# Query projection parts in every second slot of a turn, and row maxima stored ahead of the rotation

## The reference

```python
q = (x @ Wq).reshape(b, n, N_HEADS, HEAD_DIM)     # 32 heads of 16
k, v = jnp.split(ctx @ Wkv, 2, axis=-1)
...
q = apply_axial_rope(q, pos_map)
k = apply_axial_rope(k, ctx_pos_map)
logits = jnp.einsum('bqhd,bkhd->bhqk', q, k) * scale
w = jax.nn.softmax(logits, axis=-1)
attn = jnp.einsum('bhqk,bkhd->bqhd', w, v)
attn = attn.reshape(b, n, N_HEADS * HEAD_DIM)
return attn @ Wout + bout
```

## Time and profile before

| | us |
|---|---|
| median of 3 runs (1388.97 to 1389.15) | 1389.12 |
| the profiled execution's own time | 1388.06 |
| span of its profile | 1386.4 |
| attention: first scores at 721.84, last value products at | 1243.5 |
| one turn with c = 1 or 2 of batches 1 and 2 | 32.4 |
| TensorE busy, of the span | 1177.1 |
| VectorE busy | 856.9 |
| ScalarE busy | 653.6 |
| GpSimd busy | 414.5 |

### The profile page before, as it was taken

The page is one execution under the profiler, slowest core; times in us unless marked ns, Lnnn a source line. Parts: engine busy times, 40 slices in busy tenths (PEclk is TensorE's granted clock), DMA queues, the critical chain, the costliest instruction groups (busy, mean ns, idle before and its releaser), DMA issues.

```text
span 1386.4 us, 16598 instructions
## 1 busy us (share of the span) xinstructions
PE 1177.1 (85%) x5316; PEld 503.8 (36%) x5317; DVE 856.9 (62%) x1324; ACT 653.6 (47%) x1146; POOL 414.5 (30%) x479
## 2 busy tenths in 40 slices
PE   5875865999889999972459998999999999888898
PEld 3443432555444444431112222322332222234443
DVE  7899875314335555414697888777877777613543
ACT  2454452555312222232436675666666656663443
POOL 2575470011132222104333342233223223102332
PEclk8988888999989999995669999999999999999999
DMA  7223123434254444319633332222222225300011
GB/s 257 92 107 122 53 99 126 163 122 140 78 181 148 148 148 148 125 72 276 148 93 85 109 89 74 89 74 75 74 89 75 85 78 70 47 1 9 31 39 46
DMA packets 106357, 141.59 MB, mean 102 GB/s; under 512 B 20788, under 2 KB 75572, under 8 KB 106280
## 3 DMA queue, kind: packets, MB, share of 16 engines
q1 hardware_dynamic: 87432, 111.37, 24.6%
q0 software_dynamic: 18368, 28.85, 8.0%
q10 hardware_dynamic: 480, 0.39, 0.1%
HBM read 97.44 MB, written 46.27 MB: 104 GB/s over the span
## 4 chain that ended last, share of the span: by engine, by line
PE 30%; DVE 8%; issue 7%; ACT 6%; POOL 2%; DMA 2%; POOLq 0%; ACTq 0%; DVEq 0%
PE PS L2596 8%; PE PS L2566 6%; PE PS L2510 5%; PE PS L2534 5%; ACT a_E L2677 4%; PE PS L2583 4%; DVE a_top L2854 3%; POOL a_K L1908 1%; DMA a_attnT<-f_y,l_pos 1%; PE PS L2137 1%; DVE a_tab L1934 1%; DVE a_early L2756 1%; PE PS L2160 1%; PE PS L2506 0%; PE PS L2527 0%
## 5 line engine op out<-in xcount | busy, mean ns | idle before, releaser
L2854 DVE TENSOR_REDUCE a_top<-PS 128x2 f32<-128x1024 f32 x256 | 308.4, 1223 | 94.7 <-PE PS L2583 90.5
L2677 ACT ACTIVATE a_E<-PS 128x512 f32<-128x512 f32 x512 | 277.7, 596 | 148.2 <-PE PS L2566 147.9
L2566 PE MATMUL PS<-a_Q,a_K 99*128 99x512 bf16 (+1 forms) x512 | 168.0, 388 | 17.9 <-ACT a_E L2677 7.8
L1366 PE MATMUL PS<-f_W,f_GT 128*128 x312 | 141.6, 597 | 0.0
L2596 PE MATMUL PS<-a_E,a_V 128*32 128x512 f32 x1024 | 139.0, 615 | 0.0
L2583 PE MATMUL PS<-a_K,a_Q 64*128 64x512 bf16 x512 | 104.5, 405 | 39.4 <-DVE a_top L2854 25.8
L2566 PEld LDWEIGHTS PS<-a_Q,a_K 99*128 99x128 bf16 (+1 forms) x512 | 44.5, 98 | 154.6 <-ACT a_E L2677 102.3
L1770 POOL TENSOR_TENSOR a_qf<-a_qf,a_tab 128x512 f32<-128x512 f32 x15 | 19.0, 1268 | 268.9 <-DVE a_swapped L2778 268.9
L1422 DVE TENSOR_TENSOR f_H<-f_SG,PS 128x256 f32<-128x256 f32 x39 | 16.4, 421 | 125.0 <-ACT f_SG L1406 125.0
L1366 PEld LDWEIGHTS PS<-f_W,f_GT 128*128 128x128 f32 x312 | 56.9, 192 | 57.3 <-issue 57.3
L2510 PE MATMUL PS<-a_xT,a_early 128*128 128x512 f32 x128 | 75.6, 689 | 2.1 <-ACT a_xT L2647 0.8
(11 more groups left out here) (364 smaller groups left out, 2005.9 us busy)
## 6 DMA issues: line engine op xcount, KB each, us to landing
f0r_raw<-in_L_ffn_W_dram SPq DMA_DIRECT2D x24, 512.0 KB, 5.0
a_K<-k_parts SPq DMA_DIRECT2D x192, 64.0 KB, 2.3
a_Q<-a_q_parts SPq DMA_DIRECT2D x186, 64.0 KB, 2.5
f_y<-f_Y SPq DMA_DIRECT2D x39, 256.0 KB, 2.0
v_units<-V SPq DMA_DIRECT2D x16, 512.0 KB, 2.8
a_V<-v_units SPq DMA_DIRECT2D x16, 512.0 KB, 3.5
k_parts<-f_k_parts SPq DMA_DIRECT2D x16, 384.0 KB, 3.3
a_q_parts<-a_parts SPq DMA_DIRECT2D x16, 384.0 KB, 2.8
```

The lines of the kernel that those rows point to most:

```text
L1366: last = nc.tensor.matmul(PS[:, 2 + k % 2, 0:2 * I], GT[k][:, c, :], W13[:, bass.ds(e, 1), c, :].rearrange("p a n -> p (a n)"), start=(c = ...
L2566: nc.tensor.matmul(PS[:, 4 + h % 2, :], K6[k][0:rows_, o, head // 2, kt * P:(kt + 1) * P], Q6[k][0:rows_, o, head // 2, :], start=True, st ...
L2677: nc.scalar.activation(E[step % 2][:, h, :], PS[:, 4 + h % 2, :], ACT.Exp).then_inc(exp_done, 1)
L2854: nc.vector.tensor_reduce(top[:, h - h % 2:h - h % 2 + 2, t], PS[:, 2 * pair:2 * pair + 2, :], AX.X, ALU.max).then_inc(maxed, 1)
```

## The change

For the turns with c = 1 to 3, the parts of `q` move from the slots 0, 1, 2, 3 to 0, 2, 4, 6, the second `o` of the unit before from 4 to 7, its `a` from 6 to 8. VectorE's swap moves from slot 5 to 8 in those turns with b of 0 or more, and in slot 7 `outs` comes before the tasks (in every turn). GpSimd stores and loads the maxima before it rotates, in all turns.

```diff
@@ jobs
             crowded = c == 0
-            for d, when in enumerate((0, 0, 1, 2) if crowded else (0, 1, 2, 3)):
+            for d, when in enumerate((0, 0, 1, 2) if crowded else (0, 2, 4, 6)):
                 add(when, "q", before(b, c, -3), d)
-            add(3 if crowded else 4, "o", before(b, c, 1), 1)
-            add(5 if crowded else 6, "a", before(b, c, 1))
+            add(3 if crowded else 7, "o", before(b, c, 1), 1)
+            add(5 if crowded else 8, "a", before(b, c, 1))
             add(9, "m", before(b, c, -1))
@@ GpSimd
             def turn(b, c):
                 for t in tiles_to_add(b, c):
                     rows.pool(pool, t)
+                unit = before(b, c, -1)
+                if is_unit(*unit):
+                    pool.wait_ge(mT_ready, n_unit(unit))
+                    row = m_rows[bass.ds(unit[0] * DC + unit[1], 1)]
+                    pool.nop(nofuse=True)
+                    pool.dma_start(row.rearrange("a h s -> (a h) s"), mT[:]).then_inc(m_stored, 16)
+                    pool.wait_ge(m_stored, n_unit(unit, 16))
...
+                    for o in range(2):
+                        pool.dma_start(Q6[unit[1]][MAX_AT[o]:MAX_AT[o] + 3, o], by_head[o]).then_inc(m_loaded, 16)
                 q = before(b, c, -3)
                 if is_unit(*q) and not is_first(q):
...
                     rotate_and_cut(nc.gpsimd, Chain(pool, steps_rotate, (n_unit(q) - 1) * ROTATE), qf[:], swapped[:], qf[:],
                                    tab[0], 1, [parts[:, i:i + 1, :] for i in range(3)], parts_ready)
-                unit = before(b, c, -1)
-                if not is_unit(*unit):
-                    load_last_stage(b, c)
-                    return
-
-                pool.wait_ge(mT_ready, n_unit(unit))
...
                 load_last_stage(b, c)
@@ VectorE
-                    at(5, swap)
+                    at(5 if c == 0 or b < 0 else 8, swap)
@@
+                    if n == 7:
+                        outs(n)
                     for fn in tasks[n]:
                         fn()
-                    outs(n)
+                    if n != 7:
+                        outs(n)
```

More of the change, by code:

```diff
@@ L2459, in turn @@
                     rows.pool(pool, t)
+                unit = before(b, c, -1)
[5 more added lines that the diff above has]
+                    pool.wait_ge(m_stored, n_unit(unit, 16))
+                    if not is_first(unit, RING):
+                        pool.wait_ge(pv_done, n_unit(unit, 8) - RING * 8)
+                    else:
+                        pool.wait_ge(ones_ready, 4 * (unit[1] + 1))
+                    pool.nop(nofuse=True)
+                    by_head = row.rearrange("a (i h o) s -> o i (a h) s", i=3, o=2)
+                    for o in range(2):
+                        pool.dma_start(Q6[unit[1]][MAX_AT[o]:MAX_AT[o] + 3, o], by_head[o]).then_inc(m_loaded, 16)
                 q = before(b, c, -3)
```

## The result

The changed kernel takes 1394.25 (median of 20 runs, 1388.67 to 1399.47) against 1389.13 (20 runs, 1384.87 to 1393.81) for the kernel before on the same chip: a ratio of 1.0033, 95% interval 1.002 to 1.0045. It is slower, by 4.6 between the means and 5.1 between the medians. The forecast was 1388.8 with a range up to 1393.0, so the time lies outside it. Later the change was timed again on another chip, beside other kernels: 1392.85 against 1390.19, ratio 1.0009 (0.9992 to 1.0026). The first number stands, and its interval leaves out no change at all; that of the second does not. So the loss is small and its size moves from comparison to comparison.

The account below looks back on a forecast made before the run. TensorE was taken as full, a turn being its slots plus waits. Terms -2.5 - 2.1 + 1.5 + 2.3 + 1.3 - 0.8 = -0.3 on the profiled 1388.06 gave 1387.8, a forecast median of 1388.8, range 1384.2 to 1393.0.

Parts of the forecast that it names:

- The regular turns: (1, 1), (1, 2), (2, 1), (2, 2), (2, 3): query parts in even slots save TensorE time, -0.50 each, -2.5 together.
- (0, 1) and (0, 2): Turns with row additions: slots gain 0.50 and a maxima pair's wait for VectorE loses 0.55, -1.05 each, -2.1 together.
- (1, 3): Turn with a 1.44 wait and a half-clock slot behind it: half of the 1.5 taken as gained, -0.8.
- (3, 1) and (3, 2): No query left to move; `o` goes to an odd slot (+0.49), `a` behind it (+0.26): +0.75 each, +1.5 together.
- (-1, 3): VectorE's swap waits for the query part in slot 6, and the later rotation meets additions: +1.3, ends -1 and +3.
- (0, 3): Turn that has row additions as well: left at 0.
- (3, 3): `es` directly behind `o` in bank 7 waits for VectorE: +2.3, between 0.5 and 3.8 (with a fall of the clock).
- rival S: The clock falls behind new gaps, in (3, 3) and once more in (0, 3) or (-1, 3): +3.8, 1392.6, chance 0.13.
- GpSimd's and SyncE's chain: Later rotation, then SyncE's stores and loads of the query's pieces, still in time for slot 8 of the next turn: nothing.
- half-clock stretches outside (0, 3) and (1, 3): Sign that the prediction is wrong: half-clock stretches coming in places other than these two turns.

Follow-up runs that it names:

- gpsimd_alone: The kernel before with only GpSimd's order changed, its store and load of the maxima moved in front of the rotation: 1389.57, ratio 0.9995.
- both_ends_old: The change, but the turns ahead of batch 0 (slots and GpSimd's order) and those of the last batch as before: 1382.31, ratio 0.9936.
- first_turns_old: The change, but ahead of batch 0 the query's parts stay in slots 0 to 3 and GpSimd rotates first: 1386.12, ratio 0.9966.
- es_apart: The change, but in (3, 3) the gate's constants are made in slot 5, `es` goes to slot 8 and `a` to slot 9: 1387.21, ratio 0.9991.
- change_again: The change itself, timed again beside other kernels on another chip, against the kernel before: 1392.85, ratio 1.0009.
- first_slots_alone: The change, but ahead of batch 0 the query's parts are in slots 0 to 3 as before, GpSimd's new order kept: 1389.25, ratio 0.9991.
- table_alone: The change without GpSimd's new order: slots moved, but GpSimd rotates in front of the maxima in every turn: 1431.02, ratio 1.0302.
- only_33_old: The change, but `o` and `a` stay in slots 4 and 6 in the turn (3, 3) alone: 1386.57, ratio 0.9972.
- last_batch_old: The change, but in the turns of the last batch `o` and `a` stay in slots 4 and 6: 1385.86, ratio 0.9976.
- ends_and_03_old: `both_ends_old` with (0, 3) as before too, slots and GpSimd's order: 1380.32, ratio 0.9926.

## Why the prediction was wrong, by its steps

The direction of every term of the sum was right; the sizes failed at both ends. The forecast's sum was -0.3, the two traces give +6.4 from the first `qf` copy on and the times +4.6.

- **The regular turns** (forecast -0.5 each): 32.40 to 31.82 or 31.81 in each of the five, -0.58. Right; slots 8 and 9 went from 3.42 to 3.58, +0.16 where I had +0.26.
- **(0, 1) and (0, 2)** (-1.05 each): 30.22 to 29.26 and 30.39 to 29.31, -0.96 and -1.08. Right.
- **(1, 3)** (-0.8): 36.23 to 34.70, -1.5. The stretch at half clock is gone. I took half of its price; but `gpsimd_alone` lost it too with the old slots and the gap of 1.44 unchanged, so the slots aren't needed for it. Whether GpSimd's order or chance took it away one trace of before can't tell.
- **(3, 1) and (3, 2)** (+1.5): +0.7 and +1.1. Right.
- **(-1, 3)** (+1.3, ends -1 and +3): its first scores come 2.9 later, counted from the first `qf` copy. **This step failed at its price.** The swap's wait was 2.01, inside the 1.1 to 2.1 that I took, and 0.85 in the one trace with the clock at full; but `cut_max`'s gain was more than used up by additions that I let wait at most 1.27 each, one GpSimd instruction, and of which one took 2.45 longer, past two of them. On VectorE the new order cost 0.9 where I had a gain of 0.9 with up to 1.27 against it.
- **(0, 3)** (0): +1.1, and +0.5 in (1, 0), in the change's trace, where the addition L1481 took 1.69 instead of 0.75 and TensorE waited 1.62, 2.12 and 1.06 for VectorE. The addition alone is not the reason. `both_ends_old`, with the change's code in this turn, runs from 814.89 to 850.35, which is 35.5 as before, with the same addition and the same long wait:

```profile
840.65 1.69 DVE L1481 SCALAR_TENSOR_TENSOR X<-a_attnT,a_tw,X 128x512 f32<-128x512 f32 x1
...
844.28 0.39 PE L2586 MATMUL PS<-a_K,a_Q 64*128 64x512 bf16 x2 [2.12 <-DVE a_top L2857]
...
850.35 0.61 PE L2569 MATMUL PS<-a_Q,a_K 99*128 99x512 bf16 x2
```

  `first_turns_old` and `es_apart` have 35.5 too, and in `change_again` the turn took 36.0 with the addition at 0.75. So the 0 holds in three of the ten traces with this code. The other seven add 0.5 to 1.1, with a later or longer stretch at half clock and a further wait for VectorE of 0.8 to 2.0 near the turn's end. I had priced neither, and why they come in one execution and not in another stays open.
- **(3, 3)** (+2.3): +4.4. The wait itself was right to 0.02. **What failed is the choice between +2.3 and the 3.8 of my own upper end:** I put the clock's fall into rival S at 0.13, although my own sum made the stand (1.66 in the trace) longer than the 1.44 behind which the earlier trace rows shows a fall. It fell in each of the six traces that have this stand (1.66 or 1.67), and cost 2.05 in three of them and about 1.0 in three, so my price of 1.5 was right in the mean and the fault was to leave it out.
- **The final projection** (not in the sum): more time at half clock in four of those six, +1.8 in three and +3.8, in part behind the projection, in `first_slots_alone`.
- **GpSimd's and SyncE's chain** (0): right, no piece of a query came late. `table_alone` shows what stood behind that zero: 41.

On the rule that I weighed: the Trainium skill, GPSIMD Engine Reference, section Key points, says that GpSimd contends with VectorE's instructions that have two SBUF inputs. Taken in full, with every such addition waiting, the sum would have been about 2 higher by my estimate, so 1.7 against the 4.6 measured. The traces agree in sign for two-input additions (0.73 to 3.18, 0.75 to 1.63 and 1.69); the bias add lost under 0.2 (2.28 to 2.44), so not every one waits. In two traces the second addition of (0, 3) stayed at 0.75 with the change's code there.

Rival S came nearest, with the fall in (3, 3) at its heart. Its other items don't fit: it denied (1, 3) any gain, and that turn gained 1.5; and it looked for a second fall in (0, 3) or (-1, 3), while the projection had one. That its 1392.6 comes within 1.65 of 1394.25 is in part luck. The prediction also called half-clock stretches outside (0, 3) and (1, 3) a sign of being wrong; but the trace of before already has one in (3, 2), so only a new one could be such a sign, and (3, 3) had it. The chance of 0.21 for slower was too low for a change whose gains I knew to 0.1 and whose losses all stood next to gaps.

## What to carry to other kernels

A table that is right in the steady turns can lose all of it in the first and last ones: sum up those turns one by one, and give them a case of their own in the table. Here conditions on `b`, in the table and in GpSimd's order, turned a ratio of 1.0033 (1.0009 in the second comparison) into 0.9936. When a sum makes a new stand of TensorE longer than one behind which the trace already shows a fall of the clock, the fall belongs in the forecast, not among the rivals. And put jobs that share a bank at least a score pair apart when another engine must empty the bank between them.

## What was not expected of the hardware

- **The clock's fall isn't decided by the gap alone.** Behind the same gap in the same TensorE instructions it kept 2.4 GHz in one execution and fell to 1.2 GHz in another: 1.44 in (1, 3) (fell before, full in `gpsimd_alone`), 1.10 in (3, 3) (full before, fell in `gpsimd_alone` and `only_33_old`). In (3, 3) it also stayed at full behind 1.26 (`last_batch_old`, `both_ends_old`) and 1.45 (`ends_and_03_old`). With 1.66 or 1.67 it fell in six traces of six, and with 0.81 followed by 0.54 and 0.64 in the only one.
- **A row addition can lose more than one GpSimd instruction's length**: 0.73 became 3.18 where it met two of them, while the five instructions of `cut_max` next to the same rotation lost 1.4 together and the four of the normalization 1.2 (1.91 to 3.12).
- **The program ahead of the attention scatters by 7.4** from execution to execution with unchanged code, more than any term of this change. Traces are therefore compared from the first `qf` copy on.
